# A third buffer for the widened keys of the two four-head attentions, and GpSimd making them two pairs ahead

## What is computed

```
q, k, v = x @ Wq.T + bq, x @ Wk.T + bk, x @ Wv.T + bv        # first: with biases, full
q, k, v = rope(x @ wq.T), rope(x @ wk.T), x @ wv.T            # second: rotated, causal
scores  = einsum('bhqd,bhkd->bhqk', q, k) * 16 ** -0.5        # h = 4 heads, 129 keys
attn    = softmax(scores)                                     # second: keys <= query only
out     = einsum('bhqk,bhkd->bhqd', attn, v) @ Wo.T
```

## Time and profile before

| | us |
|---|---|
| median of the runs | 3343.57 |
| profiled execution, its own time | 3340.73 |
| its span | 3338.9 |
| PE busy | 3045.4 (91%) |
| DVE busy | 2144.7 (64%) |
| ACT busy | 1768.1 (53%) |
| POOL busy | 1174.2 (35%) |
| pair loop of the first attention | about 1465 to 1612 |
| pair loop of the second attention | about 1712 to 1863 |

### The profile page before, as it was taken

How to read it: one execution, slowest core, us unless ns; L and a number is a source line. 1 busy time by engine, 2 the same in 40 slices (tenths; PEclk the granted TensorE clock), 3 DMA queues, 4 the chain that set the end, 5 groups by cost and what they waited for, 6 DMA issues and landing times. The chain is left out here.

```text
span 3338.9 us, 60593 instructions
## 1 busy us (share of the span) xinstructions
PE 3045.4 (91%) x22307; PEld 1885.5 (56%) x22307; DVE 2144.7 (64%) x4177; ACT 1768.1 (53%) x3895; POOL 1174.2 (35%) x1167
## 2 busy tenths in 40 slices
PE   7999989999999999989888889996799999989999
PEld 6999857446465554357455533334466566655444
DVE  7999745016364553358568544445899999965777
ACT  1323245665756566556525433334566666655666
POOL 4666511001010011027257322223677777750000
PEclk9999989999999999999999999997899999999999
DMA  2000000000000000000000032210100000003776
GB/s 88 15 20 11 1 19 12 1 7 2 7 4 4 4 5 6 2 7 2 9 1 1 25 65 56 56 33 16 25 12 5 4 5 5 4 16 37 72 67 65
DMA packets 75645, 66.40 MB, mean 20 GB/s; under 512 B 20502, under 2 KB 70840, under 8 KB 74936
## 3 DMA queue, kind: packets, MB, share of 16 engines
q1 hardware_dynamic: 75352, 62.52, 11.0%
HBM read 55.58 MB, written 2.51 MB: 17 GB/s over the span
## 5 line engine op out<-in xcount | busy, mean ns | idle before, releaser
L707 ACT ACTIVATE p_hidden<-p_hid_ps,net_bias 128x344 f32<-128x344 f32 x816 | 382.7, 549 | 230.5 <-PE p_hid_ps L654 171.4
L680 PE MATMUL p_y_ps<-p_hidden,net_down 128*64 128x344 f32 x1632 | 287.8, 466 | 2.1 <-DVE p_hidden L756 1.9
L654 PE MATMUL p_hid_ps<-xn,net_up 64*128 64x344 f32 x1248 | 242.3, 490 | 8.1 <-PEq L316 4.6
L2785 DVE TENSOR_TENSOR p_hid<-p_silu,p_pair_ps 128x344 f32<-128x344 f32 x288 | 134.7, 509 | 172.9 <-PE p_pair_ps L2734 95.1
L756 DVE TENSOR_TENSOR p_hidden<-p_hidden,p_row 128x344 f32<-128x344 f32 x384 | 175.3, 513 | 78.3 <-ACT p_hidden L707 45.1
L2766 ACT ACTIVATE p_silu<-p_pair_ps 128x344 f32<-128x344 f32 x288 | 116.0, 454 | 201.3 <-PE p_pair_ps L2723 201.3
L1919 POOL TENSOR_TENSOR p_rot<-p_rot,p_cross 128x512 f32<-128x512 f32 x128 | 160.4, 1275 | 126.5 <-DVE p_cross L2074 126.5
L2470 POOL TENSOR_TENSOR p_qt<-p_qt,p_q_sum 97x512 f32<-97x512 f32 (+1 forms) x44 | 46.4, 1054 | 445.3 <-DVE p_q_sum L2413 445.3
L680 PEld LDWEIGHTS p_y_ps<-p_hidden,net_down 128*64 128x64 f32 x1632 | 103.7, 136 | 160.3 <-issue 49.5
L1932 POOL TENSOR_TENSOR p_prob<-p_prob,p_total 128x1024 f32<-128x1024 f32 (+1 forms) x128 | 185.5, 1470 | 12.4 <-DVE p_total L2100 12.4
L2712 POOL TENSOR_TENSOR p_weighted<-routed_hn,p_row 128x344 f32<-128x344 f32 x96 | 88.9, 946 | 262.0 <-PE p_pair_ps L2739 206.5
(11 more groups left out here) (475 smaller groups left out, 7978.2 us busy)
## 6 DMA issues: line engine op xcount, KB each, us to landing
p_row<-gated_rows SPq DMA_DIRECT2D x192, 86.0 KB, 2.9
p_row<-mark_rows SPq DMA_DIRECT2D x192, 86.0 KB, 10.6
tok_x<-in_tok_x SPq DMA_DIRECT2D x11, 384.0 KB, 3.1
out<-h SPq DMA_DIRECT2D x12, 172.0 KB, 3.4
shared_value_pairs<-shared_values SPq DMA_DIRECT2D x16, 128.0 KB, 2.5
p_swapped<-xn SPq DMA_DIRECT2D x64, 32.0 KB, 1.9
p_x<-in_tok_x SPq DMA_DIRECT2D x5, 384.0 KB, 3.1
p_kinds<-in_tok_c3w SPq DMA_DIRECT2D x1, 1280.0 KB
```

Source lines behind the costliest of these rows:

```text
L654: mm = pe.matmul(hid_ps[k % ring][:, 0:TILE], w_up[half(g), n, :], x[half(g), cols(t)], start=True, stop=not experts or by_rows)
L680: mm = pe.matmul(y_ps[u][half(g), 0:TILE], w_down[:, n, :], hid[k % hidden_ring][:], start=n == 0, stop=last and not experts)
L707: act.activation(hid[k % hidden_ring][:], hid_ps[k % ring][:, 0:TILE], func, bias=b_up[:, n:n + 1]).then_inc(act_done.sem, 1)
L2785: dve.tensor_tensor(hid[n % ring_h][g][:], silu[n % 2][g][:], c_of(n, g)[:, 0:TILE], ALU.mult).then_inc(hid_ready.sem, 1)
```

## The change

`k_wide` gets a third buffer. GpSimd widens the keys of pairs 0 and 1 ahead of its loop and in step j those of pair j+2. From pair 3 on it waits for the scores of the pair three before, where it waited from pair 2 on for those of the pair two before. TensorE reads buffer j % 3. It holds for both attentions.

```diff
-        k_wide = [ph.sb(f"k_wide{r}", [P, HEADS, seen]) for r in two]
+        k_wide = [ph.sb(f"k_wide{r}", [P, HEADS, seen]) for r in range(RING3)]
...
-                                      k_wide[j % 2][half(g), :, :], start=False, stop=True).then_inc(scored.sem, 1)
+                                      k_wide[j % RING3][half(g), :, :], start=False, stop=True).then_inc(scored.sem, 1)
...
-                                           k_wide[j % 2][half(g), 2 * c:2 * c + 2, :], start=True, stop=True)
+                                           k_wide[j % RING3][half(g), 2 * c:2 * c + 2, :], start=True, stop=True)
...
                 def widen_keys(j):
-                    if j >= 2:
-                        pool.wait_ge(scored.sem, scored.at(HALVES * (j - 1)))
+                    if j >= RING3:
+                        pool.wait_ge(scored.sem, scored.at(HALVES * (j - RING3 + 1)))
                     keys = slice(j * SEQ, j * SEQ + seen)
-                    pool.tensor_tensor(k_wide[j % 2][:], k[:, None, keys].to_broadcast([P, HEADS, seen]),
+                    pool.tensor_tensor(k_wide[j % RING3][:], k[:, None, keys].to_broadcast([P, HEADS, seen]),
...
                 widen_keys(0)
+                widen_keys(1)
                 for j in range(PAIRS + 1):
-                    if j + 1 < PAIRS:
-                        widen_keys(j + 1)
+                    if j + 2 < PAIRS:
+                        widen_keys(j + 2)
```

## The result

The changed kernel takes 3324.71 us (median of 11 runs, 3316.09 to 3330.26) against 3342.09 us for the kernel before (11 runs, 3333.25 to 3370.57). The ratio is 0.9941, with a 95% interval of 0.9918 to 0.9963, so 0.4% to 0.8% faster. The forecast of 3333.0 us had the direction and lay too high; its range ended at 3326, 1.3 us above the result.

The account below looks back on a forecast made before the run. No engine is full; the chain between engines, with keys arriving last every second pair, was taken to bound both attention loops. 5.7 + 6.0 - 1.1 = 10.6 us off 3343.6 gave 3333.0 us, range 3326 to 3341.

Parts of the forecast that it names:

- The chain through the long step: Pair loops: alternate steps between VectorE's maxima, 4.68 and 5.19 us, wait for scores, held by keys GpSimd widens late.
- the recurrence with one wait for two pairs: Maximum starts at the later of D(j-1) + 3.85 and D(j-2) + 8.53 us; a removed wait gains once per two pairs.
- the place of the keys in GpSimd's queue: Keys come late behind the previous pair's scaling and values' copy; moved one pair ahead, TensorE's wait goes to 0.
- GpSimd's new wait: Widening waits for the scores of the pair three before; semaphore already given by then, price 0.
- The third widening at the start: Start of each attention: about 1 us more of GpSimd where it would stand idle; price 0, bounds 0 to 0.8 us.
- The other semaphore: VectorE's lowering, which the scores also wait for, given a microsecond before; otherwise nothing gained, 3343 to 3344 us, chance 0.07.
- the lower clock: Rival slower: earlier scores lengthen or repeat TensorE's low clock, 2.1 us a pair, 3354 us for 10 pairs; chance 0.03.
- The term that was too small: Scores' wait for the keys in both attentions goes to 0, gaining 5.7 and 6.0 us.
- long steps of 4.27 and 4.73 us: Sign of being right: long step between VectorE's maxima in the first and second attention after the change.
- the 1.1 us given back in the short step: First attention: second turning waits for GpSimd's scaling, giving back 0.08 us 14 times.
- The upper bound of the waits, 12.1 us: Both attentions: nothing given back and every key wait at its longest, 14 x 0.4 + 13 x 0.5 us.
- The rival "more": Second attention's low-clock stretch goes with the keys' wait: 1.4 us more, 13.5 us in all, 3330 us; chance 0.10.

Follow-up runs that it names:

- E5: Kernel before, with GpSimd widening the keys ahead of the copy of the values instead of behind it; 3329.51 us against 3337.44 (0.9975).
- E9: Kernel before, with TensorE's scores put ahead of the turning from pair 3 on, two buffers, keys one pair ahead; 3334.74 us against 3341.96 (0.9978).
- e4: Kernel before, with keys widened two pairs ahead in both attentions but only two buffers; 3320.59 us (0.9939).
- e3: Kernel before, with the third buffer alone in both attentions, keys still widened one pair ahead; 3335.28 us against 3338.05 (0.9987).

## Why the prediction was right and wrong

**Right.** The chain through the long step, the recurrence with one wait for two pairs, and the place of the keys in GpSimd's queue. E5 confirms the recurrence in a second dose (6.5 us for 0.25 us of earliness, where one gain for every pair would have been 13). E9 confirms that in the kernel before nothing but the keys closed the period. GpSimd's new wait costs nothing: even in e4, whose wait is for the scores of a later pair, it shows only among the first pairs. The third widening at the start cost nothing either: it took 1.05 us, and D(0) of the first attention came 4.25 us after the first widening began, before and after. The other semaphore was not as late, and the lower clock did not grow.

**The term that was too small** is "14 x 0.41 = 5.7 us in the first attention, 13 x 0.46 = 6.0 us in the second". The idle time ahead of the scores' matmul is not what the wait cost. In the kernel before, L1062 began at these times in the two long steps:

```profile
1544.19 0.29 PE L1062 MATMUL p_o_ps<-p_end_t,p_val 128*128 128x8 f32 x2
```

```profile
1780.88 0.29 PE L1062 MATMUL p_o_ps<-p_end_t,p_val 128*128 128x8 f32 x2
```

From there to the scores it took 1544.88 - 1544.19 = 0.69 us and 1781.62 - 1780.88 = 0.74 us. In the changed kernel, with nothing to wait for, the next matmul begins 0.22 us (1547.78 to 1548.00) and 0.14 us (1782.07 to 1782.21) after L1062 begins, although the record of L1062 runs for 0.29: the recorded end of one matmul is later than the moment at which the next may start. So the idle time shown begins 0.07 and 0.15 us too late. The wait cost 0.47 and 0.60 us, and the periods fell by 0.48 and 0.61. In the first attention that is 14 x 0.48 = 6.7 us, as measured (115.62 - 108.95); in the second 13 x 0.61 = 7.9, and 0.4 more in the one step at low clock, 8.3 as measured. The forecast had 5.7 and 6.0. Its long steps of 4.27 and 4.73 us came out as 4.20 and 4.58.

The distance from L1062 to the scores was the thing to read, but not in the short step, although no wait is shown there. In the kernel before:

```profile
1784.34 1.05 POOL L1133 TENSOR_TENSOR p_k_wide<-p_k,L2f_of_head 128x512 f32<-128x512 f32 x1
...
1785.17 0.29 PE L1062 MATMUL p_o_ps<-p_end_t,p_val 128*128 128x8 f32 x2
```

The scores begin at 1785.44, 0.27 us after L1062, and that would have priced the long step's wait at 0.47 us, hardly more than the 0.46 shown. But the widening ends at 1784.34 + 1.05 = 1785.39, 0.05 us ahead of the scores, the same lag as in the long step (1544.83 to 1544.88). TensorE waits for the keys here too, by 0.13 us, and the record of L1062 hides it. My reading of this step as free of that wait was wrong; it cost nothing, since VectorE sets the short step. A distance that nothing held stood just after the low stretch, before L1025 at 1745.59:

```profile
1745.45 0.29 PE L1062 MATMUL p_o_ps<-p_end_t,p_val 128*128 128x8 f32 x2
```

That is 0.14 us, and with it the second attention's wait would have been 0.60. The first attention has no such place ahead of L1033 in the kernel before: its shortest distance is the 0.27 us of its short step, which would have priced the wait at 0.42 us.

**The term that should not be there** is the 1.1 us given back in the short step. The second turning of that step does now stand right behind the scaling (1540.88 + 2.05 = 1542.93, turning at 1542.99), as the step foresaw. But the short step is set by VectorE: with the scores at 1543.77 they would release a maximum at 1544.94 (1.17 us later, as in the long step), and VectorE began it at 1544.97, with no idle time before it. My own recurrence, with the later of two terms, says that a delay under this slack costs nothing; I added it to the sum all the same.

Together: 14.8 us in the attentions in place of 10.6. **The rest of the miss** is the level. I set the sum against the median of three runs, 3343.6 us, one of them at 3367.2; the result's section puts the comparable median at 3340.0. Of the 8.3 us by which the forecast lay too high, 4.2 are the attentions, 3.6 this level, and 0.5 can't be placed. The upper bound of the waits, 12.1 us, was below the true 14.8 because it came from the same kind of row: the longest idle time is not a bound on what a wait costs if the record before it ends late.

**The low clock.** The rival "more" expected that the low stretch of the second attention might go with the keys' wait. It did not go. The same pair, j = 5, has it in the changed kernel, although its wait for the keys is gone:

```profile
1730.44 1.01 PE L1025 MATMUL p_wide_ps<-later,place 128*128 128x512 bf16 x2
...
1735.49 0.59 PE L1025 MATMUL p_wide_ps<-later,place 128*128 128x512 bf16 x2
```

Ahead of the turning of this step TensorE had stood 1.43 us in the kernel before and 1.44 in the changed one; the granted clock is 0.51 in 1738.8:1745.4 and 0.57 in 1729.5:1733.5, close to the lower level. The stretch is shorter after the change: from this L1025 to the next it is 5.05 us and was 6.58. Yet against the executions without a low stretch in the steady part it costs D no less: 1.4 us in the kernel before (123.72 against 122.36 in e3) and 1.6 in the changed one (115.37 against 113.75 in e4). It is no part of the gain.

## What to carry to other kernels

Find the period of a loop by the starts of one instruction, and see over how many turns it repeats; here a chain spans two turns, and a wait in it is won once for two. Price a wait by the distance between the starts of the same two instructions where nothing holds the second, not by the idle time ahead of the waiting one. That no wait is shown is not enough: check that what the second one needs ended well before it starts, or take the shortest such distance in the trace, and call the price a lower bound where none is free. Before adding a buffer, ask whether the producer is late because its buffer is taken or because of what stands ahead of it in its queue: here moving it in the queue was all, and it also opened the way for an order of TensorE that alone had not moved the period.

## What the runs showed of the hardware

The record of L1062, 128x8 in two parts, runs for 0.29 us, but the next matmul starts sooner after it when nothing holds it: 0.14 us ahead of L1025 and 0.22 us ahead of L1033. A span of 0.29 us of "busy" TensorE thus holds 0.07 to 0.15 us in which it could have started the next, and in which a wait does not show. I had read these rows as if an engine were occupied to the end of its record. TensorE starts 0.05 us after the end of the widening that it waits for, shown (1544.83 to 1544.88) or hidden (1785.39 to 1785.44), and this lag gives a hidden wait away.
